# First weight unit in pieces, output blocks moved ahead of the last key projections, first maxima ahead of batch 2's projections

## What is computed

```
x_proj = einsum('btc,dc->btd', x, w_in);  xi, gate = split(x_proj, 2)
h = silu(causal_conv_4_taps(xi) + b) * D * silu(gate)
x = layernorm(x + h @ w_out.T)

q = x @ Wq.T;  k, v = split(ctx @ Wkv_expand.T, 2)        # 16 heads of 32
x = layernorm(x + softmax(causal(q k.T / sqrt(32))) v @ Wout.T)

y = top-2-of-8 experts(x) + shared expert(x)
x = layernorm(x + y)
```

## Time and profile before

| | |
|---|---|
| median of 3 runs | 1165.55 us (1164.60 to 1170.72) |
| time of the profiled execution | 1167.04 us |
| its span, first to last instruction | 1165.1 us |
| TensorE (PE) busy | 1074.1 us, 92% of the span |
| VectorE, ScalarE, GpSimd busy | 687.1, 456.8, 281.3 us |
| mean granted TensorE clock | 0.966 of full speed |

### The profile page before, as it was taken

The page is one execution under the profiler, slowest core; times in us unless marked ns, Lnnn a source line. Parts: engine busy times, 40 slices in busy tenths (PEclk is TensorE's granted clock), DMA queues, the critical chain, the costliest instruction groups (busy, mean ns, idle before and its releaser), DMA issues. The chain is left out here.

```text
span 1165.1 us, 19181 instructions
## 1 busy us (share of the span) xinstructions
PE 1074.1 (92%) x6790; PEld 904.8 (78%) x6790; DVE 687.1 (59%) x1518; ACT 456.8 (39%) x807; POOL 281.3 (24%) x368
## 2 busy tenths in 40 slices
PE   6899999997849999999779879999999999899997
PEld 4688888885738888887657669999999899777784
DVE  3746466474145676776254656777777677344475
ACT  4523324153105444554353145555555455221210
POOL 4510100221203333333344021122211110323030
PEclk9999999999966999999989889999999999999999
DMA  4403040213495788874271266667666675524141
GB/s 148 177 1 108 0 186 3 62 47 135 130 255 132 202 240 225 233 208 107 74 240 54 75 215 223 237 223 240 232 241 244 227 229 166 168 73 138 42 151 65
DMA packets 90708, 179.35 MB, mean 154 GB/s; under 512 B 8128, under 2 KB 37568, under 8 KB 88864
## 3 DMA queue, kind: packets, MB, share of 16 engines
q1 hardware_dynamic: 83984, 155.06, 43.0%
q0 software_dynamic: 6672, 23.60, 6.0%
HBM read 136.95 MB, written 41.42 MB: 153 GB/s over the span
## 5 line engine op out<-in xcount | busy, mean ns | idle before, releaser
L45 PE MATMUL e_ps_h<-e_x_lo,e_gu_hi 128*128 128x256 f32 (+1 forms) x552 | 155.9, 282 | 5.0 <-DVE e_x_lo L1918 5.0
L46 PE MATMUL e_ps_h<-e_x_hi,e_gu_lo 128*128 128x256 f32 (+1 forms) x552 | 153.9, 279 | 0.0
L47 PE MATMUL e_ps_h<-e_x_hi,e_gu_hi 128*128 128x256 f32 (+1 forms) x552 | 153.7, 278 | 0.0
L45 PE MATMUL a_ps_proj<-a_x_lo,arena 128*128 128x512 f32 x272 | 109.8, 404 | 17.8 <-DVE a_x_lo L350 11.6
L923 DVE CUSTOM_DVE_ANT_0 b_dump<-b_ps_s,b_mask 128x128 f32<-128x128 f32 (+1 forms) x256 | 80.5, 354 | 58.1 <-PE b_ps_s L1098 56.4
L46 PE MATMUL a_ps_proj<-a_x_hi,arena 128*128 128x512 f32 x272 | 109.2, 401 | 0.0
L47 PE MATMUL a_ps_proj<-a_x_hi,arena 128*128 128x512 f32 x272 | 109.2, 401 | 0.0
L45 PEld LDWEIGHTS e_ps_h<-e_x_lo,e_gu_hi 128*128 128x128 f32 (+1 forms) x552 | 99.4, 180 | 6.3 <-DVE e_gu_lo L1922 5.2
L46 PEld LDWEIGHTS e_ps_h<-e_x_hi,e_gu_lo 128*128 128x128 f32 (+1 forms) x552 | 99.6, 180 | 0.9
L369 DVE SCALAR_TENSOR_TENSOR a_xc<-a_ps_proj,a_taps,a_xc 128x510 f32<-128x510 f32 (+2 forms) x96 | 71.6, 746 | 48.6 <-ACT a_xc L313 46.4
L47 PEld LDWEIGHTS e_ps_h<-e_x_hi,e_gu_hi 128*128 128x128 f32 (+1 forms) x552 | 99.5, 180 | 0.0
(11 more groups left out here) (321 smaller groups left out, 2649.2 us busy)
## 6 DMA issues: line engine op xcount, KB each, us to landing
f_gate_up_raw<-we_gate_up SPq DMA_DIRECT2D x88, 352.0 KB, 4.9
b_sk<-qk_split SPq DMA_DIRECT2D x48, 256.0 KB, 4.5
b_sq<-qk_split SPq DMA_DIRECT2D x48, 256.0 KB, 6.0
qk_split<-arena SPq DMA_DIRECT2D x24, 512.0 KB, 6.1
f_down_raw<-we_down SPq DMA_DIRECT2D x23, 512.0 KB, 6.9
y_slots<-f_y_tile SPq DMA_DIRECT2D x23, 512.0 KB, 2.8
f_x_next<-x SPq DMA_DIRECT2D x7, 1024.0 KB, 5.7
f_down_raw<-we_down SPq DMA_DIRECT2D x23, 192.0 KB, 6.8
```

The lines of the kernel that those rows point to most:

```text
L45: pe.matmul(out, a_hi, b_lo, start=first, stop=False)
L46: pe.matmul(out, a_lo, b_hi, start=False, stop=False)
L47: return pe.matmul(out, a_hi, b_hi, start=False, stop=last)
```

## The change

Three places are changed.

1. Start. The first weight unit is loaded as four pieces of 128 KB, each right behind the x chunk of the same number. ACT rounds the piece and the chunk, DVE makes both rests (POOL did the unit's before), and block 0 is multiplied chunk by chunk, both sides of a chunk together, each as soon as its rest is there. Inside group 0 the two weight units of a block are no longer rounded back to back, but one behind the gate and one behind the block's second Silu.
2. End of the convolution. The order ahead is now transposes, keys, queries, and the first two of the eight output blocks come before them.
3. Start of attention. The first scores stand in front of the queries of batch 2, whose matmuls are put between them; ACT and DVE follow the same order. On SP `load_peaks(0, 0)` moves ahead of the four stores.

```diff
@@ -165,7 +165,8 @@
         k_hi, k_lo, q_hi = (arena[:, (5 + k) * DC * D:(6 + k) * DC * D].rearrange("p (c t) -> p c t", c=DC)
                             for k in range(3))
         q_lo = x_raw[:].bitcast(F32R)
-        AHEAD = [("k", c) for c in range(DC)] + [("x", c) for c in range(DC)] + [("q", c) for c in range(DC)]
+        AHEAD = [(kind, c) for kind in ("x", "k", "q") for c in range(DC)]
+        BEFORE = 2
 
         def ahead_bank(n):
             return ps_proj[:, n // 2 % 2, n % 2]
@@ -194,15 +195,15 @@
         @block.sync
         def _(sp):
             for c in range(DC):
+                at = slice(c * 2 * P, (c + 1) * 2 * P)
                 sp.dma_start(x_raw[:, c], x_t[0][:, c]).then_inc(chunk_loaded[c], 16)
-                if c == 0:
-                    sp.dma_start(w_raw[:, 0], w_in[0]).then_inc(w_loaded[0], 16)
+                sp.dma_start(w_raw[:, 0, at], w_in[0][:, at]).then_inc(chunk_loaded[c], 16)
+            sp.dma_start(w_raw[:, 1], w_in[1]).then_inc(w_loaded[1], 16)
             sp.dma_start(taps[:], conv_w).then_inc(consts_loaded, 16)
             sp.dma_start(bias[:], conv_b).then_inc(consts_loaded, 16)
             sp.dma_start(dgain[:], gain).then_inc(consts_loaded, 16)
-            for u in range(1, W_UNITS):
-                if u >= 2:
-                    sp.wait_ge(w_lo_done, u - 1)
+            for u in range(2, W_UNITS):
+                sp.wait_ge(w_lo_done, u - 1)
                 src = w_in[u] if u < JC else w_out[u - JC]
                 sp.dma_start(w_raw[:, u % 2], src).then_inc(w_loaded[u % 2], 16)
             sp.wait_ge(first_lo_done, DC)
@@ -234,11 +235,12 @@
             sp.dma_start(xt[:], x_tok[LAST]).then_inc(xt_loaded, 16)
             for u in range(W_UNITS + 2, ALL_UNITS):
                 load_following(u)
-            sp.wait_ge(ahead_lo_done, 1 + DC)
+            sp.wait_ge(ahead_ready, DC)
+            sp.wait_ge(ahead_lo_done, 1)
+            load_next(1)
+            sp.wait_ge(ahead_lo_done, 1 + 2 * DC)
             store_ahead(0, k_hi)
             store_ahead(1, k_lo)
-            sp.wait_ge(ahead_ready, 2 * DC)
-            load_next(1)
             sp.wait_ge(ahead_lo_done, 1 + 3 * DC)
             store_ahead(2, q_hi)
             store_ahead(3, q_lo)
@@ -258,11 +260,13 @@
 
             pool.memset(ln.power[:], -0.5).then_inc(ln_const, 1)
             def split_w(u):
-                pool.wait_ge(w_hi_done, u + 1)
+                pool.wait_ge(w_hi_done, u)
                 pool.tensor_tensor(w_unit(u, False), w_raw[:, u % 2], w_unit(u, True).bitcast(F32),
                                    ALU.subtract).then_inc(w_lo_done, 1)
 
-            for u in range(W_UNITS):
+            pool.wait_ge(first_lo_done, DC)
+            pool.sem_inc(w_lo_done, 1)
+            for u in range(1, W_UNITS):
                 split_w(u)
             pool.memset(ident[:], 0.0).then_inc(ln_const, 1)
             pool.wait_ge(ln_const, 2)
@@ -293,15 +297,14 @@
                 act.activation(h_hi[:, j], hf[:, j % 2], ACT.Copy).then_inc(h_hi_done, 1)
 
             def split_w(u):
-                act.wait_ge(w_loaded[u % 2], 16 * (u // 2) + 16)
+                act.wait_ge(w_loaded[u % 2], 16 * ((u + 1) // 2))
                 act.activation(w_unit(u, True), w_raw[:, u % 2], ACT.Copy).then_inc(w_hi_done, 1)
 
+            act.sem_inc(gate_free, BANKS)
             for c in range(DC):
-                act.wait_ge(chunk_loaded[c], 16)
+                act.wait_ge(chunk_loaded[c], 32)
+                act.activation(wi_hi[:, 0, c].rearrange("p s m -> p (s m)"), w_raw[:, 0, c * 2 * P:(c + 1) * 2 * P], ACT.Copy)
                 act.activation(x_hi[:, c], x_raw[:, c], ACT.Copy).then_inc(x_hi_done, 1)
-                if c == 0:
-                    split_w(0)
-            act.sem_inc(gate_free, BANKS)
             for u in range(1, W_AHEAD):
                 split_w(u)
             act.wait_ge(consts_loaded, 48)
@@ -314,8 +317,8 @@
                                    scale=taps[:, j, TAPS - 1:TAPS], bias=bias[:, j:j + 1]).then_inc(tap_last, 1)
                     act.activation(sg[:, j % 2], ps_proj[:, j % 2, 1], ACT.Silu).then_inc(gate_free, 1)
                     if isinstance(g, int) and g == 0:
-                        for u in range(W_AHEAD + 2 * j, min(W_AHEAD + 2 * j + 2, W_UNITS)):
-                            split_w(u)
+                        if W_AHEAD + 2 * j < W_UNITS:
+                            split_w(W_AHEAD + 2 * j)
                     if isinstance(g, int) and g == LAST:
                         if j == 2:
                             act.wait_ge(consts_loaded, 48 + 32)
@@ -327,6 +330,8 @@
                         h_round(g, j - 1)
                     act.wait_ge(conv_done, BANKS + JC * g + j + 1)
                     act.activation(xcj, xcj, ACT.Silu).then_inc(silu_done, 1)
+                    if isinstance(g, int) and g == 0 and W_AHEAD + 2 * j + 1 < W_UNITS:
+                        split_w(W_AHEAD + 2 * j + 1)
                 h_round(g, JC - 1)
 
             group(0)
@@ -347,6 +352,8 @@
             dve.sem_inc(conv_done, BANKS)
             for c in range(DC):
                 dve.wait_ge(x_hi_done, c + 1)
+                dve.tensor_tensor(wi_lo[:, 0, c].rearrange("p s m -> p (s m)"), w_raw[:, 0, c * 2 * P:(c + 1) * 2 * P],
+                                  wi_hi[:, 0, c].rearrange("p s m -> p (s m)").bitcast(F32), ALU.subtract)
                 dve.tensor_tensor(x_lo[:, c], x_raw[:, c], x_hi[:, c].bitcast(F32), ALU.subtract).then_inc(first_lo_done, 1)
             dve.wait_ge(consts_loaded, 48)
 
@@ -406,18 +413,24 @@
             def project(g):
                 pe.wait_ge(x_lo_done, g)
                 for j in range(JC):
-                    pe.wait_ge(w_lo_done, j + 1)
-                    for side, free in ((0, conv_done), (1, gate_free)):
-                        pe.wait_ge(free, JC * g + j + 1)
-                        for c in range(DC):
-                            mm = three_pass(pe, ps_proj[:, j % 2, side], wi_hi[:, j, c, side], wi_lo[:, j, c, side],
-                                            x_hi[:, c], x_lo[:, c], c == 0, c == DC - 1)
+                    if j:
+                        pe.wait_ge(w_lo_done, j + 1)
+                        order = [(side, c) for side in range(2) for c in range(DC)]
+                    else:
+                        order = [(side, c) for c in range(DC) for side in range(2)]
+                    for side, c in order:
+                        if c == 0:
+                            pe.wait_ge(gate_free if side else conv_done, JC * g + j + 1)
+                        if j == 0 and side == 0:
+                            pe.wait_ge(first_lo_done, c + 1)
+                        mm = three_pass(pe, ps_proj[:, j % 2, side], wi_hi[:, j, c, side], wi_lo[:, j, c, side],
+                                        x_hi[:, c], x_lo[:, c], c == 0, c == DC - 1)
                     mm.then_inc(proj_done, 1)
 
-            def output(g):
+            def output(g, first, end):
                 pe.wait_ge(w_lo_done, W_UNITS)
                 pe.wait_ge(out_free, TILES * g)
-                for j in range(JC):
+                for j in range(first, end):
                     pe.wait_ge(h_lo_done, JC * g + j + 1)
                     for t in range(TILES):
                         mm = three_pass(pe, ps_out[:, t], h_hi[:, j, t * P:(t + 1) * P], h_lo[:, j, t * P:(t + 1) * P],
@@ -447,21 +460,21 @@
...
                 if kind == "q":
                     if c == 0:
-                        pe.wait_ge(ahead_lo_done, 1 + 2 * DC)
+                        pe.wait_ge(ahead_lo_done, 1 + DC)
                         pe.wait_ge(w_lo_done, W_UNITS + 3)
...
-            pe.wait_ge(first_lo_done, DC)
             with pe.Fori(0, LAST) as g:
                 project(g)
-                output(g)
+                output(g, 0, JC)
             project(LAST)
+            output(LAST, 0, BEFORE)
             for n, (kind, c) in enumerate(AHEAD):
                 ahead(n, kind, c)
-            output(LAST)
+            output(LAST, BEFORE, JC)
 
 
 HEADS = 16
@@ -690,6 +703,8 @@
                     load_peaks(t, 1)
                 if real(b + 2):
                     load_inputs(b + 2)
+                if t < 0:
+                    load_peaks(0, 0)
                 if real(b):
                     store_k(b, 0)
                     store_q(b, 0)
@@ -701,8 +716,6 @@
                     load_peaks(t + 1, 0)
                 if real(b):
                     store_q(b, 1)
-                if t < 0:
-                    load_peaks(0, 0)
                 if 2 <= t < B:
                     load_res(t)
@@ -862,9 +872,14 @@
                 cs = slice(UC * u, UC * u + UC)
                 act.activation(a_hi[:, cs], a_raw[:, cs], ACT.Copy).then_inc(a_hi_done, 1)
 
+            values(0, 0)
+            values(0, 1)
+            context(GB)
+            turned(GB, 0)
+            turned(GB, 1)
             for u in range(2):
```

(35 more changed lines are left out.)

## The result

| | before | changed |
|---|---|---|
| median | 1166.07 us | 1148.35 us (1146.72 to 1152.31) |
| ratio, 95% interval | | 0.9846 (0.9808 to 0.9884) |
| profiled execution, its span | 1167.04, 1165.1 us | 1147.71, 1145.7 us |
| TensorE busy | 1074.1 us | 1073.2 us |

The change makes the kernel 1.5% faster, 17.7 us by the medians and 19.4 by the spans of the two profiled executions. The forecast was 1145.6 (1141 to 1152). TensorE's work is the same; what went is waiting, and some work at the lower clock.

A forecast was written before the change was run, and what follows sets the result against it. TensorE, busy for 92% of the span, was taken as the bound, so gains come from its idle or low-clock time. 6.0 + 8.8 + 5.1 = 19.9 us less gave a median of 1145.6 us, range 1141 to 1152.

The forecast's parts named there:

- Start, 6.0 forecast: Start through group 0: gain of 6.0 us, bounds 4.0 and 7.0, from an earlier TensorE start and fewer waits.
- the walk through the weights: Group 0, followed unit by unit: projections end at 56.1 against 63.1, a gain of 7.0 us.
- a piece of 128 KB costs 0.5: Start: each piece of the first weight unit adds 0.5 us of loading; chunk and piece 0 are there at 4.4.
- the prediction's own sign of being wrong: Group 0: the forecast is wrong if TensorE waits over 3 us in total in blocks 3 to 7.
- The cycle of a slot: Group 0 weights: load, round and rest take 6.8 us for two units, against 5.5 for a block of 24 matmuls.
- The start alone gives 5.0: Start: TensorE beginning at 6.6, 5.0 us earlier, gives 5.0 us by itself.
- the second rival: One part gives nothing: rows still land at 350, or weights hold group 0; total 14 to 15 us; 11 in 100.
- End of the convolution, 8.8 forecast: End of the convolution: waits and low clock go, 9.1 less 0.3 gives 8.8 us, bounds 7.3 and 9.1.
- Attention, 5.1 forecast: Start of attention: rows pass four stores of 2.1 MB and land at 345.2, 5.1 us earlier; bound above 5.7.
- The first rival: Start of attention: clock falls in the 4.8 us idle before the stack; third part gives 2.8, total 17.6; 14 in 100.
- The slower case: From attention on: clock, down at 320, stays down past 390 and eats the gain; 5 in 100.
- the other two: Rivals: one part gives nothing, 1151 us, 11 in 100; nothing gained as a later stage has its own date, 1165.5, 5.

The follow-up runs named there:

- e9: e8 with the weight units going through four slots in place of two; median 1136.65 us, ratio 0.9738.
- e5: Start part alone on the kernel before, but ScalarE's two weight-unit splits of a block stay together as before; median 1163.70 us, ratio 0.9974.
- e4: Kernel before with only the load of half 0's rows moved ahead of batch 2's four stores on SP; median 1161.27 us, ratio 0.9955.
- e6: Changed kernel with batch 2's queries and second keys again ahead of the scores of half 0; median 1148.95 us, ratio 0.9849.
- e7: Changed kernel with the load of half 0's rows moved ahead of the last stack load on SP; median 1149.57 us, ratio 0.9864.
- e2: Only the end-of-convolution part on the kernel before; median 1159.29 us, ratio 0.9933.
- e8: e7 with two queries before the scores, other projections placed anew, half 1's rows ahead of half of batch 2's stores; median 1142.31 us, ratio 0.9800.

## Why the prediction was right, and where it was off

**The sum.** 19.9 us were forecast, the stage means give 18.6, the spans 19.4; the medians say 17.7 (13.5 to 22.4 by the interval), a little under the 18 to 22 that had 65 in 100. The mechanisms hold: all three parts count, and they add up within what the runs can tell. The end of the convolution is the largest, as forecast; the start was to be the second and came third.

**Start, 6.0 forecast, 4.8 measured.** The first matmul near 6.6 is right (6.88, in the other profiles with the new start 6.1 to 6.7). The term that was mis-sized is the walk through the weights, which had "read" at 56.1; in the six profiles it is 57.2 to 58.0, 57.6 in the mean. The walk gave 7.0 us: 1.5 of them it missed so, and 0.7 were never there, since the one profile of before that it started from was late at this point (63.2, 62.4 in the mean of four). Two of its numbers were off. The first is in "a piece of 128 KB costs 0.5" and "the bytes up to the fourth chunk are the same": the fourth piece is taken at 9.23, 1.0 us later than the fourth chunk of before (8.60 to 9.33 in the nine profiles with pieces), so unit 2's load, which needs all four rests, went out at 11.3 and not 10.5, and unit 4 reached ACT at 21.44, not 20.6. From the Trainium skill's figure for transfers of 64 KB (DMA: Bandwidth & Descriptors, section Bandwidth; there issued from GpSimd, here by SP) the prediction had an estimate of 2 us for the pieces and didn't take it over. The trace shows half of that, so taking nothing was wrong. Whether the lower rate costs it is not shown: SP also issues the last of the eight loads at 4.19, where the last chunk's was out by 3.2 before, and no run parts the two. Second, two waits of 0.6 and 1.2 us for taps were left by the walk, and there are four, 2.7 us in all; in the five other profiles with this start 3.0 to 3.2. So the prediction's own sign of being wrong, over 3 us of waits in these blocks, was only just missed. The cycle of a slot, 6.8 us for two units, was read rightly (6.87, 6.78, 6.76), and so was its weight: that it makes the waits is what e9 shows. By e5 the front alone is worth 2.1, where the prediction said "The start alone gives 5.0": without the splits' places most of what the second rival says, that the weights hold group 0, would have come true.

**End of the convolution, 8.8 forecast, 8.5 measured.** It is 9.0 from group 3's last read on, less the 0.5 that the groups lost and no term held. No wait, clock 1.00, and 38.4 us from the last projection's end (259.1) to the last output's (297.5), where 38.6 were forecast.

**Attention, 5.1 forecast, 5.3 measured.** The rows pass 2.1 MB of stores, and e4 shows that this alone does it. The first profile's 6.2 us was one execution with quicker loads; without it the stage gives 4.8. The rows and not the scores end last, as forecast.

**Rivals.** The first rival's event came true and its price didn't fall due: the clock fell in the wait for the stack, the 12 projection matmuls behind it were 0.21 apart and not 0.12, and it was back near 312. The Trainium skill's rule (TensorE: Matmul & The Clock Gate, Part 1: The HAM clock gate) said that this fall comes, and the trace agrees (0.50 behind the wait of 4.13 us). Its other half, that sustained work releases the clock, fails here later on: from 340.5 to 349.0 TensorE was busy for 8.49 of 8.50 us at 0.50. But the scores ended at 328.3, 2.5 us ahead of the rows. e6, where the clock stays up until 317, has the same time. The slack is real but small: in e7, without the loads ahead of the rows, the scores end last, in a profile in which the clock fell twice. The slower case didn't come: the clock was back at 350, not past 390. Neither did the other two.

**Left open.** The stage means give 18.6 and the medians 17.7; 0.9 us is less than the interval can tell. From "picks" on the profiles scatter by 4 us (813.3 to 817.3, and 818.6 in e7, whose wait for half 1's rows lies there), most of it in code that no part touches; what adds a stretch at the low clock there in e2, e5, e6, e7 and e9, and what makes a middle group 0.4 us longer, was not tried.

## What to carry to other kernels

When a load is late, count the bytes that its own queue holds ahead of it before moving the work that produces it: here one moved load on SP was worth as much as that move and the new order on three engines together. But a load that waits for its data holds up all behind it, as e7's did. Moving an engine's start forward pays only up to the next thing with a cycle of its own; price that cycle (slot free, load, round, rest) first, and give it a slot more before warming clocks. Compare stages over all profiles with the same code there: one profile's stage is good to about 1 us.

## What the runs showed of the hardware beside

- The rate of the same stack loads was 242 GB/s in one profiled execution of the changed kernel and 221 to 230 in the twelve others (stretches of 16 to 20 us).
- A rest on DVE (two operands in SBUF) takes 2.48 us beside POOL's own rest and 0.68 when POOL is idle (e9, at 35.03 and at 46.15, POOL's last rest being done by 42.6), while the three taps, which read PSUM, take 2.31 either way. The Trainium skill's SBUF — State Buffer, section Terms, tells of a port pair that the two engines lock for a whole instruction; both numbers fit, and no run tried it by itself.
- In the scores and picks of the changed kernel the clock was at 0.50 for 24 us, the last 8.5 of them with TensorE counted as busy throughout (rows above); it came back at 350, as late behind the first picks (19 us) as before (from 350 to 369).
- The length of the wait for the stack alone doesn't tell whether the clock falls: e8's fell at 309, behind a wait of 1.33 us for the stack, and before it stayed up until 331, behind one of 1.69 us.
- The view's granted clock says 1.00 from the start of the program on, also where matmuls of 512 columns follow each other at 0.43 us; they do so at 0.23 from 11.97 on. There the level is read from the steps:

```profile
7.00:9.00 2.00, 2.00 (x5) 1.61 (x6) 1.03 (x2) 1.20 (x3) 0.00 (x0) 1.00 0.98 363
```
